# A two-layer feature-interaction tower: layer 1's pair products from DRAM factors instead of squares on chip

## The reference

```
x1[b,s,d] = relu( sum_{h,m} x0[b,h,d] * x0[b,m,d] * W1[s,h,m] + b1[s] )     s < 128
x2[b,s,d] = relu( sum_{h,m} x1[b,h,d] * x0[b,m,d] * W2[s,h,m] + b2[s] )     h < 128, m < 39
z = concat(x1.sum(d), x2.sum(d), dense_ctx)
y = relu(relu(z @ W_top1 + b) @ W_top2 + b) @ W_top3
```

## Time and profile before

| | |
|---|---|
| median of 3 runs | 1174.59 us (1174.16 to 1176.11) |
| the profiled execution | 1172.96 us, span 1171.2 us, mean granted TensorE clock 0.985 |
| TensorE busy | 1137.7 us, 97% |
| VectorE busy | 1068.0 us, 91% |
| GpSimd busy | 895.7 us, 76% |
| ScalarE busy | 688.0 us, 59% |
| DMA | 12.00 MB, 170,381 packets, mean 10 GB/s |
| chain that ended last | TensorE 93%, VectorE 3%, issue 2% |

### The profile page before, as it was taken

The page is one execution under the profiler, slowest core; times in us unless marked ns, Lnnn a source line. Parts: engine busy times, 40 slices in busy tenths (PEclk is TensorE's granted clock), DMA queues, the critical chain, the costliest instruction groups (busy, mean ns, idle before and its releaser), DMA issues.

```text
span 1171.2 us, 19309 instructions
## 1 busy us (share of the span) xinstructions
PE 1137.7 (97%) x4942; PEld 907.8 (78%) x4942; DVE 1068.0 (91%) x3821; ACT 688.0 (59%) x2167; POOL 895.7 (76%) x930
## 2 busy tenths in 40 slices
PE   4699999999999999999999999999999999999998
PEld 2377777888887888888888777888888888888876
DVE  4268889999999999999999888999999999999976
ACT  3365555666665666666666556666766666667542
POOL 6388989888888888889889767888887546555542
PEclk9599999999999999999999999999999999999998
DMA  6101111111111111111111110111111000000000
GB/s 200 6 3 7 7 7 7 7 7 7 8 7 7 8 7 6 8 7 7 7 7 7 6 6 4 7 7 7 8 7 6 1 1 1 1 1 1 1 1 1
DMA packets 170381, 12.00 MB, mean 10 GB/s; under 512 B 163630, under 2 KB 169262, under 8 KB 170141
## 3 DMA queue, kind: packets, MB, share of 16 engines
q1 hardware_dynamic: 160029, 8.13, 7.8%
q0 software_dynamic: 10240, 2.64, 2.9%
HBM read 8.31 MB, written 0.00 MB: 7 GB/s over the span
## 4 chain that ended last, share of the span: by engine, by line
PE 93%; DVE 3%; issue 2%; POOL 1%; ACT 1%; DMA 0%; POOLq 0%; SPq 0%; ACTq 0%; DVEq 0%
PE ps L941 24%; PE ps L942 24%; PE ps L945 24%; PE ps L895 4%; PE ps L913 3%; PE ps L908 3%; PE ps L909 3%; PE ps L911 3%; PE ps L975 3%; DVE acc L823 2%; PE ps L883 1%; POOL looked L449 1%; PE ps L952 1%; PE ps L902 1%; PE ps L1031 0%
## 5 line engine op out<-in xcount | busy, mean ns | idle before, releaser
L823 DVE SCALAR_TENSOR_TENSOR acc<-ps,e,acc 128x128 f32<-128x128 f32 x3186 | 852.4, 344 | 42.1 <-PE ps L945 30.5
L941 PE MATMUL ps<-w2h,x1h 128*128 128x512 f32 (+1 forms) x1280 | 514.7, 402 | 2.4 <-DVE acc L823 0.9
L458 POOL TENSOR_TENSOR fy<-fy 128x512 f32<-128x512 f32 (+1 forms) x256 | 402.6, 1573 | 145.8 <-ACT fy L583 131.3
L942 PE MATMUL ps<-w2l,x1h 128*128 128x512 f32 (+1 forms) x1280 | 495.6, 387 | 0.0
L945 PE MATMUL ps<-w2h,x1l 128*128 128x512 f32 (+1 forms) x1280 | 493.8, 386 | 0.0
L583 ACT ACTIVATE fy<-ps,e 128x128 f32<-128x128 f32 x1536 | 415.7, 389 | 65.0 <-PE ps L945 61.7
L449 POOL DMA_INDIRECT looked<-in_table,rows x320 | 307.6, 961 | 68.6 <-issue 37.0
L941 PEld LDWEIGHTS ps<-w2h,x1h 128*128 128x128 f32 x1280 | 241.5, 189 | 65.2 <-DVE acc L823 7.9
L942 PEld LDWEIGHTS ps<-w2l,x1h 128*128 128x128 f32 x1280 | 241.1, 188 | 51.7 <-issue 7.6
L945 PEld LDWEIGHTS ps<-w2h,x1l 128*128 128x128 f32 x1280 | 240.8, 188 | 48.7 <-DVE x1l L769 0.7
L615 ACT ACTIVATE zh<-ps 128x512 fp32r<-128x512 f32 x156 | 96.3, 617 | 177.6 <-PE ps L895 173.9
(11 more groups left out here) (93 smaller groups left out, 660.5 us busy)
## 6 DMA issues: line engine op xcount, KB each, us to landing
e<-looked SPq DMA_DIRECT2D x360, 5.0 KB, 1.9
looked<-in_table,rows POOLq DMA_INDIRECT x320
e<-looked SPq DMA_DIRECT2D x120, 4.5 KB, 1.9
w_st<-in_w SPq DMA_DIRECT2D x1, 1728.0 KB
wt_sb<-in_wt SPq DMA_DIRECT2D x2, 512.0 KB
w_st<-in_w SPq DMA_DIRECT2D x1, 768.0 KB, 6.0
w_sb<-in_w1a SPq DMA_DIRECT2D x1, 448.0 KB
w1b_sb<-in_w1b SPq DMA_DIRECT2D x1, 448.0 KB
```

Source lines behind the costliest of these rows:

```text
L458: nc.gpsimd.tensor_tensor(out, a, b, ALU.add).then_inc(s_fsum, 1)
L823: nc.vector.scalar_tensor_tensor(acc[:, sub, :] if m < fields("D", last)[-1] else y, y, emb(p, sub, m), acc[:, sub, :] if m else fsum[:, p ...
L941: nc.tensor.matmul(y, x1h[:, t % 2, at], w2h[:, cols], start=True, stop=False)
L942: nc.tensor.matmul(y, x1h[:, t % 2, at], w2l[:, cols], start=False, stop=False)
```

## The change

Layer 1's products are now made from factors rather than by squaring sums. SP writes each tile's gathered rows to DRAM (`fields_d`, 39 fields, the first 20 twice), and reads back e for layer 2 with one transfer. For each of six chunks v of 128 pairs it reads both factors of every row: `ab[:, v, 0]` and `ab[:, v, 1]`, 128x512 each (`fetch`, 4 or 5 transfers a chunk). One elementwise product (`product`) on VectorE (chunks 0, 2, 3, 4) or GpSimd (chunks 1 and 5, in tiles above 2; `by_pool`) gives the multiplication's operand. TensorE does one full-precision multiplication per chunk in every tile. Twelve pairs per position are still multiplied out directly; their high and low parts go to DRAM (`pairs_d`) and come back turned (`keep_pairs`, `by_pair`), ScalarE copies them to float32r (`to_pass`), and one pass adds them, last. Positions are now numbered b-major, so ScalarE and VectorE read the accumulator with strides.

Gone are the selection, the squares and their splits, the fold of the weights, the transposes, `e_hl` and the low part of e, and layer 1's use of the staging bank. Forty gathers (was 35) come ahead of the loop, and then 6 and 5 alternate (was 6 from pair 4 on). The MLP weights are loaded during tile 2.

```diff
-ZP = 15
+ZP = 12
-LOOKUPS_FIRST, LOOKUPS_NEXT = 3 * LOOKUPS, 5
+LOOKUPS_FIRST, LOOKUPS_NEXT = 4 * LOOKUPS, 0
+POOL_CHUNKS = (1, 5)
+AHEAD, AHEAD_FIRST = 6, 3
+SECOND_PRODUCTS = {0: (0,), 1: (1,), 2: (2,), 3: (3,), 4: (4, 5)}
+ACT_FETCHES = (3, 4, 5)
+LAYER1_AT = (6, 9, 11, 14, 16, 19, 21)
+LAYER1_SECOND = (9, 11, 13, 15, 17, 19, 21)
+def by_pool(t, v):
+    return t > FIRST_TILES and v in POOL_CHUNKS
 def lookups(p):
-    return 6 if p == 0 or p >= 4 else 5
+    return 6 - p % 2
...
+        def product(engine, t, v):
+            engine.wait_ge(s_ab[v], 16 * len(segments(v)) * (t + 1))
+            engine.tensor_tensor(ab[:, v, 0, :], ab[:, v, 0, :], ab[:, v, 1, :], ALU.mult).then_inc(
+                s_z_pool if by_pool(t, v) else s_z_dve, 1)
+        def fetch(engine, t, v):
+            engine.wait_ge(s_kept[t], 3 * 16)
+            if t:
+                engine.wait_ge(s_mm1, C1 * (t - 1) + v + 1)
+            for row, count, h, shift in segments(v):
+                first = (t * X_ROWS + h) * N
+                engine.dma_start(ab[row:row + count, v, :, :], bass.AP(fields_d.tensor, first, [[N, count], [shift * N, 2], [1, N]])
+                                 ).then_inc(s_ab[v], 16)
...
+                for t in range(2, TILES):
+                    for v in range(C1):
+                        if v == 0 and t > 2:
+                            keep_pairs(t - 1)
+                        fetch(sp, t, v)
+                        if v == 1 and t > 2:
+                            by_pair(t - 1)
+                        if v == 3 and t + 1 < TILES:
+                            keep_fields(t + 1)
+                        if v == 4 and t + 1 < TILES:
+                            by_position(t + 1)
...
                     look_ahead(1)
-                    if mine is not None and not mine_soon:
-                        low_parts(nc.gpsimd, mine)
+                    for at in pool_products(p):
+                        product(nc.gpsimd, *at)
+                    if (soon := SPLIT_IN.get(p + 1)) is not None:
+                        multiplied_out(nc.gpsimd, soon)
...
-                        for at in split_after(p, j):
-                            square_low(*at)
+                        for at in products_after(p, j):
+                            product(nc.vector, *at)
...
+                def layer1_at(t, v):
+                    if v == C1:
+                        pe.wait_ge(s_zt, t + 1)
+                        pe.wait_ge(s_wz, 1)
+                        nc.tensor.matmul(ps[:, BK_ACC1, :], wz[:], zt[:, t % 2, :], start=False, stop=True).then_inc(s_mmz, 1)
+                        return
+                    if v == 0 and t:
+                        pe.wait_ge(s_x1l, t)
+                    pe.wait_ge(s_z_pool if by_pool(t, v) else s_z_dve, products_made(t, v))
+                    nc.tensor.matmul(ps[:, BK_ACC1, :], w1_sb[:, v, :], ab[:, v, 0, :], start=(v == 0), stop=False).then_inc(s_mm1, 1)
```

More of the change, by code:

```diff
@@ L35, with segments @@
 LOOKED = 8
-HELD = 4
-SOON = 6
 SHIFTS = (M + 1) // 2
-ZP = 15
+ZP = 12
 K1 = P
[L47 to L53, removed]
+FULL = K1 // M
+C1 = (SHIFTS * M - ZP) // K1
+REST = [(C1 * FULL + k // M, k % M) for k in range(C1 * (K1 - FULL * M))]
+ZH0, ZM0 = M - ZP, SHIFTS - 1 - ZP
+assert REST[-1] == (SHIFTS - 1, ZH0 - 1) and C1 * K1 + ZP == SHIFTS * M
+ZG = ZP + 1
+ZROWS = 3 * ZG
+TWICE = 20
+X_ROWS = M + TWICE
+def segments(v):
+    runs = [(M * k, M, 0, FULL * v + k) for k in range(FULL)]
+    row, n = M * FULL, K1 - M * FULL
+    for shift, pairs in itertools.groupby(REST[n * v:n * (v + 1)], key=lambda pair: pair[0]):
+        pairs = list(pairs)
+        runs.append((row, len(pairs), pairs[0][1], shift))
+        row += len(pairs)
+    return runs
 MB = 4
@@ new lines, in layer1_steps, with products_made, products_after @@
+def layer1_steps(p, s):
+    return layer1_slot(SLOTS * p + s)
+def by_pool(t, v):
+    return t > FIRST_TILES and v in POOL_CHUNKS
+def products_made(t, v):
+    mine = by_pool(t, v)
+    return sum(by_pool(u, w) == mine for u in range(t + 1) for w in range(C1) if (u, w) <= (t, v))
+def products_after(p, j):
+    slots = [s for s, kind in enumerate(ORDER) if kind == "D"] + [SLOTS]
+    steps = [(1, v) for v in SECOND_PRODUCTS.get(j, ())] if p == 0 else []
+    for ahead, tiles in ((AHEAD_FIRST, (2,)), (AHEAD, range(3, TILES))):
+        steps += [at for s in range(slots[j], slots[j + 1]) for at in layer1_slot(SLOTS * p + s + ahead) if at[0] in tiles]
+    return [(t, v) for t, v in steps if v < C1 and not by_pool(t, v)]
@@ L197, with pool_products, z_step @@
+def pool_products(p):
+    return [(t, v) for s in range(1, SLOTS + 1) for t, v in layer1_slot(SLOTS * (p + 1) + s) if v < C1 and by_pool(t, v)]
+SPLIT_IN = {2 * t - 4: t for t in range(FIRST_TILES, TILES)}
+HIGH_SLOT = 2
+def z_step(p, s):
+    at = {4: 1} if p == 0 else {}
+    at.update({4: t} if (t := SPLIT_IN.get(p - 1)) is not None else {})
+    return at.get(s)
 CALM = 4
 def lookups(p):
-    return 6 if p == 0 or p >= 4 else 5
-def high_slots(p):
-    return (6, 7) if p == 0 else (4, 5) if p == 2 else (1, 4) if SPLIT_IN[p] < SOON else (3, 6)
+    return 6 - p % 2
@@ new lines, in by_pair @@
+                def by_pair(t):
+                    sp.wait_ge(s_zw, 16 * (t + 1))
+                    if t:
+                        sp.wait_ge(s_zt, t)
+                    sp.dma_start(z_raw[:], pairs_d[t, :, :]).then_inc(s_zr, 16)
+                keep_fields(0)
+                by_position(0)
+                for v in range(C1):
+                    if v not in ACT_FETCHES:
+                        fetch(sp, 0, v)
+                keep_pairs(0)
+                keep_fields(1)
+                by_pair(0)
@@ new lines, in _ @@
+                by_position(1)
+                for v in range(C1):
+                    fetch(sp, 1, v)
+                keep_pairs(1)
+                keep_fields(2)
+                by_pair(1)
+                by_position(2)
+                for t in range(2, TILES):
+                    for v in range(C1):
+                        if v == 0 and t > 2:
[7 more added lines that the diff above has]
+                            by_position(t + 1)
+                        if t == 2 and v == 5:
+                            for dst, src in mlp_weights:
+                                sp.dma_start(dst, src).then_inc(s_mlpw, 16)
@@ L439, in _ @@
+                keep_pairs(TILES - 1)
+                by_pair(TILES - 1)
                 sp.wait_ge(s_tail, 7)
@@ L549, in _ @@
                     look_ahead(1)
-                    if mine_soon and p != 2:
+                    if mine is not None:
                         low_parts(nc.gpsimd, mine)
```

413 lines of the change are left out of this document (132 added, 281 removed).

## The result

The kernel after takes 1280.4 us (median of 4 runs, 1277.39 to 1286.2), the kernel before 1174.38 beside it (1172.96 to 1176.11): ratio 1.0907, 95% interval 1.087 to 1.0943. Slower, as forecast, but by 106 us where 9 were forecast, and far outside the range of 1148 to 1206. The profiled execution took 1277.39 with a span of 1275.4, 104.2 more than the span of 1171.2 before.

What follows compares the result with a forecast made beforehand. GpSimd, full beside TensorE and VectorE, was to pace gather tiles at 34.2 us. Start -5, MLP tiles -3 and -1.5, gather tiles +13.3, collisions +7.6, late tiles -2: +9.4 on 1172.96, 1182.4, forecast 1184; range 1148 to 1206.

Steps and rivals of the forecast that it cites:

- I count nothing on the path: DMA queues and SP's issue: 21 of 34 us a tile, fetches with 14 slots of time, so no cost added.
- three more transfers' latency: DMA, each tile: the bounds set on the added cost, 0 to 3 us.
- worth nothing: ScalarE, each tile: loses about 8 of 21.25 us of work, but had 12 us free, so no gain.
- rival 4: Round trip over DRAM late: TensorE waits 1 to 3 us each tile, 45 us in all, 1225; chance 0.08.
- Start, -5: Start up to VectorE's pair 7: 5 us earlier, between -12 and +3, with GpSimd fixing the time.
- GpSimd's own load of 34.2: GpSimd, gather tiles: 33.35 + 2.50 - 0.48 - 1.16 = 34.2 us, above TensorE, VectorE and the old 33.50.
- Collisions, +0.4 a tile: GpSimd, gather tiles: pushed back by VectorE's two-operand SBUF products, 0.4 us a tile, +7.6 over 19 tiles.
- rival 3: Collisions at their upper end: 19 x 1.0 more, VectorE +2 in the last tiles, 1205; chance 0.14.
- VectorE, 32.1 before collisions: VectorE, each tile: loses six `zl`, gains four products, 33.3 becomes 32.1 us; 1.5 of waiting makes 33.6.
- Late tiles, -2: 4.5 tiles after the gathers: TensorE's -0.8 each, mostly eaten by VectorE's collisions; -2 us (-4 to +1).
- TensorE, 32.7: TensorE, tiles from 6 on: loses 5.99 us, gains 5.16, so -0.83 and 32.7 us a tile.
- MLP tiles, -4.5: Three tiles with the MLP's first group: -3 us as TensorE-bound, -1.5 for the lead GpSimd regains there.

Runs made afterwards that it cites:

- a2: Kernel after, without storing and bringing back the kept products; the pass reads rows of `fields_d` instead, so their share is left out: 1236.78 us.
- b4: Kernel after, with `pairs_d` written in rows of 624 bytes and the 16-byte pieces picked apart when read back: 1242.1 us.
- a4: Kernel after, with `e` brought by 16 transfers from SBUF to SBUF instead of one read from DRAM: 1307.41 us.
- c1: Kernel after, with the twelve kept pairs fetched as a seventh chunk (no store and return) and the MLP weights loaded three tiles later: 1219.11 us.
- b1: a1 with VectorE's factor products cut to 8 of 512 columns, the rest left out: 1216.26 us.
- a1: Kernel after, with ScalarE's copy of the kept products moved four slots later: 1253.87 us.
- c3: a1 with all factor products, VectorE's and GpSimd's, cut to 8 of 512 columns, the rest left out: 1198.15 us.
- c2: c1 with a third product of each tile moved from VectorE to GpSimd from tile 28 on: 1214.19 us.

## Why the prediction was wrong

- **DMA, "I count nothing on the path": the step that failed.** The volume was right (14.2 us a tile against 15). The small pieces were priced at 9 ns from a row of SBUF to SBUF; written to DRAM they took 42. With 5,008 of them a tile that is 13 us of 16 engines where 3 were counted, and their issue holds up the sync engine as well: the DMA engines are 89% busy in a gather tile, and the trip of the kept products takes 18.7 us. It was bounded as "three more transfers' latency", 0 to 3 us, and I named as queued behind it the fetches, which had slack. I did not look at who stands behind the wait on ScalarE, the engine I had written off with "worth nothing": its `fy` has no slack. Without the trip the span is 40.7 us shorter (a2): 22.2 in the start and 19.1 in the 28 tiles. In the tiles this is rival 4's mechanism, at 0.67 a tile instead of 1.5 (its sum, 45 on 1182.4, gives 1227 and not the 1225 written). The Trainium skill, DMA: Bandwidth & Descriptors, section "Specifications", speaks against pieces under 512 B, and the prediction gave that rule a chance of 0.08. Runs a2 and b4 bear it out for the store; reading such pieces was cheap here (a4: 4 ns more than from SBUF, some 13).
- **Start, -5: measured +45.9 at pair 7.** The 40 gathers ended at 54.2, as forecast (55). But I took GpSimd as what fixes the start and its inputs as ready. Up to 180 us it waited 33.3 us for ScalarE's `fy` (17.2 before) and 11.7 for `e`; without the trip these fall to 18.1 and 3.7. Without the trip the start is 22 us shorter (a2), with the seventh chunk and the late MLP weights 29 (c1), of 35.9 at tile 3. TensorE stood meanwhile, at a granted clock of 0.50 and 0.59, so its first work ran at or near 1.2 GHz. The rest is open: in c1 the mark of tile 3 is still 7 us late, and pair 7, which does not depend on the mark's earlier slot, 12 (199.78 against 187.70). From 100 us on VectorE is busy 19.8 to 19.9 of 20 us in c1 and 16.4 to 19.7 before; what would win back its lead was not tried.
- **GpSimd's own load of 34.2: borne out** by b1, where its work is not pushed: 30.72 busy and 3.3 of gaps, mostly issue, in a tile of 34.0. The agreement to the digit is partly luck, since b1's chain runs over TensorE and VectorE. That GpSimd paces in the kernel after is only part of it: it had 21% of the chain there and 24% in a1.
- **Collisions, +0.4 a tile: mis-sized.** They are 1.5 (35.68 - 34.20), above the bound of 1.4 that I gave and past the 0.9 from which rival 3 decides. I took a third of the pushes as felt. In the rows shown the wait of VectorE ended only when GpSimd's reads had a gap, GpSimd's own adds of two operands are pushed (`xs` by 0.36, `fy` with bias by 0.14 twice a tile), and so are gathers (mean 1.00 to 1.02, and 0.96 in b1). The Trainium skill, SBUF — State Buffer, section "Who interferes with whom", has the first half: two SBUF inputs of VectorE against any read of GpSimd. It keeps descriptor writing out of it. The gathers of b1 and c3 (0.96) against a1 (1.02) do not settle that, nor does the 1.55 of the prediction: a gather also reads its row numbers from SBUF.
- **VectorE, 32.1 before collisions.** With the product at 0.68 minus overlap, c3's last tile gives 30.59 - 4 x 0.31 + 4 x 0.62 = 31.8, near it. With collisions it is 34.1 in a1, 2.3 of waiting where 1.5 was estimated. So the cover that I named for it (below GpSimd's) is gone where gathers end.
- **Late tiles, -2: measured +5 in four tiles** (34.77 against 33.51), VectorE's by collisions: b1 has 33.3 there, and c2, moving one product, gains 1.1 a tile in the last three.
- **TensorE, 32.7: 33.1.** Only -0.4 of 33.5 is left of the gain. Even with nearly free products (c3) 28 tiles gain 13 us.
- **MLP tiles, -4.5.** Tiles 16 to 20 take 151.1 before, 160.2 after, 154.2 in a1, 151.0 in c3: no gain in any of them.

In one line, over 28 tiles: TensorE -13.4 (c3 less before), products and collisions +57.4 (a1 less c3), ScalarE standing behind the trip +18.8 (after less a1): 62.8.

## What to carry to other kernels

Before work is moved from an engine to DMA, price the small pieces in the direction in which they go, on the DMA engines and on the engine that issues them, and follow every wait for their landing to the queue of the engine that makes it: what stands behind that wait, not the waiting instruction, is the cost. An elementwise operation with two SBUF operands on VectorE is priced with what GpSimd does at the time; where GpSimd is nearly full, both engines pay, here 1.5 us a tile on one and 2.3 on the other for 2.7 us of products. And a gain of 0.8 of 33.5 us on the pacing engine needs every other engine's term to be right to a few tenths.

## What the hardware showed that I had not expected

- A 16-byte piece took 42 ns of a DMA engine when written from SBUF to DRAM (a2), some 15 when picked out of DRAM (b4), and 9 from SBUF to SBUF.
- A VectorE product of 8 columns took 0.15 us at its shortest and had a mean of 0.57 beside a busy GpSimd (b1): the wait, not the size, was its price. Of 512 columns the longest in a1 took 2.85 us.
- A transfer in some 5,000 pieces makes the next issue long: 4.13 us in the mean behind the store of `pairs_d`, 2.96 behind the read of `e`, 0.39 behind a fetch, and 0.34 behind the same store in rows of 624 bytes (b4). With the backlog of the start it was 11.25.
- The float32r pass of 39 rows and the one behind it took 0.43 each on the chain instead of 0.23 (c3).
